# The latents' attention of a four-block network: where the first values and the last output projections are computed

## The reference

```python
h = jnp.concatenate([x, latents], axis=1)
q = (x @ q_w + q_b).reshape(b, 512, NH, DH)
kv = (h @ kv_w + kv_b).reshape(b, 576, NH, DH, 2)
kmat, v = (kv[..., 0], kv[..., 1])
attn = jnp.einsum('bkhd,bnhd->bhkn', q, kmat) / DH
attn = jax.nn.softmax(jnp.where(mask, attn, -inf), axis=-1)
attn_out = jnp.einsum('bhkn,bnhd->bkhd', attn, v).reshape(b, 512, H)
attn_out = attn_out @ out_w + out_b + residual
# then root mean square norm, an MLP with 2048 hidden channels, and the residual
```

## Time and profile before

| | us |
|---|---|
| median of three runs | 2801.22 (2800.64 to 2805.96) |
| the profiled execution | 2802.86, its span 2800.8 |
| TensorE busy | 2650.6 (95%) |
| VectorE busy | 1450.7 (52%) |
| ScalarE busy | 781.3 (28%) |
| GpSimd busy | 389.2 (14%) |
| mean granted TensorE clock | 0.98 of full speed |

### The profile page before, as it was taken

One profiled execution on the slowest core, in us unless ns is written; L12 is line 12 of the kernel. 1 busy time (PEld: TensorE's weight loads), 2 busy tenths in 40 slices (PEclk: granted clock), 3 DMA queues, 4 the chain that ended last, 5 costly groups with the idle time before them and its releaser, 6 DMA issues. The chain is left out here.

```text
span 2800.8 us, 30410 instructions
## 1 busy us (share of the span) xinstructions
PE 2650.6 (95%) x12328; PEld 1929.1 (69%) x12328; DVE 1450.7 (52%) x2282; ACT 781.3 (28%) x1363; POOL 389.2 (14%) x282
## 2 busy tenths in 40 slices
PE   9999999999899999879999999979999888899999
PEld 7778777877678888635444444358888766578887
DVE  6465566555763443435445454475334497763443
ACT  4322233223321110215344352430111143331110
POOL 0000000000220000014344342422000220220000
PEclk9999999999999999989999999899999999999999
DMA  4100110010100000321212122120000100100001
GB/s 190 60 31 32 59 61 31 32 60 1 64 1 31 31 1 1 135 56 45 52 39 64 49 49 55 33 106 32 18 16 0 68 1 0 52 14 30 31 1 60
DMA packets 35604, 118.28 MB, mean 42 GB/s; under 512 B 8069, under 2 KB 8198, under 8 KB 25994
## 3 DMA queue, kind: packets, MB, share of 16 engines
q1 hardware_dynamic: 35466, 116.35, 12.6%
HBM read 81.18 MB, written 7.34 MB: 32 GB/s over the span
## 5 line engine op out<-in xcount | busy, mean ns | idle before, releaser
L1549 DVE TENSOR_REDUCE l_top<-l_slot 128x1 f32<-128x512 f32 x256 | 170.3, 678 | 192.6 <-PE l_slot L1360 191.8
L1499 ACT ACTIVATE l_weighed<-l_across 128x512 f32<-128x512 f32 (+1 forms) x320 | 183.0, 594 | 298.1 <-PE l_across L1382 294.2
L389 PE MATMUL l_wide<-l_key_map,l_norm 128*128 128x260 f32 x1024 | 235.3, 383 | 2.7 <-ACT l_norm L544 2.3
L389 PEld LDWEIGHTS l_wide<-l_key_map,l_norm 128*128 128x128 f32 x1024 | 191.8, 190 | 32.1 <-ACT l_norm L544 2.7
L1230 POOL TENSOR_TENSOR l_paired<-l_weighed 128x2048 f32<-128x2048 f32 x32 | 145.5, 4548 | 397.2 <-ACT l_weighed L1499 337.0
L1382 PE MATMUL l_across<-l_q_stack,l_k_stack 99*128 99x512 f32 (+1 forms) x320 | 186.9, 588 | 11.8 <-ACT l_weighed L1499 8.8
L725 DVE TENSOR_TENSOR x<-l_added,x 128x512 f32<-128x512 f32 x128 | 87.0, 687 | 82.3 <-PE l_added L131 60.6
L1382 PEld LDWEIGHTS l_across<-l_q_stack,l_k_stack 99*128 99x128 f32 (+1 forms) x320 | 59.1, 186 | 97.0 <-issue 61.8
L1360 PE MATMUL l_slot<-l_k_stack,l_q_stack 97*128 97x512 f32 x256 | 112.0, 438 | 14.4 <-DMA l_k_stack<-l_k_parts 6.2
L2337 ACT ACTIVATE l0m_hidden<-l0m_up,columns 128x512 f32<-128x512 f32 x64 | 44.2, 692 | 271.7 <-PE l0m_up L131 259.6
L2337 ACT ACTIVATE l3m_hidden<-l3m_up,columns 128x512 f32<-128x512 f32 x64 | 44.2, 692 | 269.9 <-PE l3m_up L131 256.7
(11 more groups left out here) (379 smaller groups left out, 5943.0 us busy)
## 6 DMA issues: line engine op xcount, KB each, us to landing
l_k_stack<-l_k_parts SPq DMA_DIRECT2D x192, 72.0 KB, 2.0
l_q_stack<-l_q_parts SPq DMA_DIRECT2D x192, 64.0 KB, 2.0
l_wk<-in_weights SPq DMA_DIRECT2D x9, 1024.0 KB, 4.9
l_wv<-in_weights SPq DMA_DIRECT2D x9, 1024.0 KB, 4.8
l_wo<-in_weights SPq DMA_DIRECT2D x9, 1024.0 KB, 4.8
l_wqT<-in_weights SPq DMA_DIRECT2D x8, 1024.0 KB, 7.0
l0m_raw<-in_weights SPq DMA_DIRECT2D x8, 1024.0 KB, 4.7
l2m_raw<-in_weights SPq DMA_DIRECT2D x8, 1024.0 KB, 4.8
```

The costliest lines, as they stand in the source:

```text
L389: last = pe.matmul(wide[:, j, 0:W], norm[:, k, at:at + P], key_map[:, k, b, :, :].rearrange("p h c -> p (h c)"), start=k == 0, stop=k == K ...
L1499: act.activation(weighed[0:height(c), (CHUNKS * g + c) % RING, j, :], across[0:height(c), use % 2, :], ACT.Exp)\
L1549: dve.tensor_reduce(top[:, t, j:j + 1], slot[:, i % 2, :], AX.X, ALU.max, negate=True).then_inc(s["top_ready"], 1)
```

## The change

- The semaphore `setup` is split in `bias_scaled` and `mask_ready`. ScalarE's first copies wait for neither; its first q take waits for the first, SyncE's first stack load for the second.
- Element 0's values no longer stand in one block. `first_values(piece)` is one product; four stand ahead of the logits of group 0, and one ahead of each of the 16 logits. They use the banks of `gathered`, `totals` and `across`, which are unused until group 0's loop. VectorE takes a chunk ahead of maxima 0, 4, 8 and 12 and the last behind maximum 15; `split(1)` moves from ahead of the maxima to behind maximum 12. The first logits wait for `k1_out` and `q_out`, the first `turn_tops` for all values.
- Element 2's output projection no longer stands between the values of element 3 and group 12's loop. `late_out` puts one product beside steps 0 to 3 and 8 to 11 of groups 13 and 14, in the bank `work`; VectorE adds behind maxima 5 and 13 of those groups. SyncE's store of these rows moves to group 14.
- Element 3's output projection puts its first twelve products beside the first 12 steps of group 15 (`last_out`), in four banks; the last four follow the last `mixed` (`finish_out`). GpSimd adds the bias for these rows in group 15, between the two pair sums, no longer in group 12.
- `mixed` has two buffers, by element.

The diff, cut to its core:

```diff
-        mixed = n.sbuf(f"{tag}_mixed", [P, GROUPS, S], F32, mem)
+        mixed = n.sbuf(f"{tag}_mixed", [P, 2, GROUPS, S], F32, mem)
...
+        FIRST_VALUE_BANK = (gathered[:, :], totals[:, :], across[:, 0, :], across[:, 1, :], gathered[:, :])
+        LAST_BANK = (slot_bank[0], slot_bank[1], slot_bank[2], work[:, :])
+        TAIL = ALL - GROUPS + 1
...
-            sp.wait_ge(s["setup"], 2)
+            sp.wait_ge(s["mask_ready"], 1)
...
-                if g % GROUPS == GROUPS - 1 and b + 1 < B:
+                if g == ALL - 2:
+                    sp.wait_ge(s["out_added"], TPB * (B - 1))
+                    sp.dma_start(n.dram["l2_rows"][:, (B - 2) * TPB:(B - 1) * TPB, :], rows[:, :, :]).then_inc(s["rows_stored"], 16)
+                elif g % GROUPS == GROUPS - 1 and b + 2 < B:
...
+                if g == ALL - 1:
+                    add_bias(b)
...
+            def first_values(piece):
+                c, k = piece // KT, piece % KT
+                if c == CHUNKS - 1 and k == 0:
+                    pe.wait_ge(s["values_out"], 1)
+                last = pe.matmul(FIRST_VALUE_BANK[c][0:height(c), :], source[:, k, keys_of(c)], wv[:, k, :], start=k == 0, stop=k == KT - 1)
+                if k == KT - 1:
+                    last.then_inc(s["values_done"], 1)
...
+            def late_out(g, step):
+                if step % 8 >= GROUPS or step >= TILES_OF:
+                    return
+                t, m = 2 * (g - TAIL) + step // 8, step % 8
+                if m == 0:
+                    if t:
+                        pe.wait_ge(s["out_added"], TPB * (B - 2) + t)
+                    else:
+                        pe.wait_ge(s["mixed_ready"], GROUPS * (B - 1))
+                        pe.wait_ge(s["k1_out"], ALL)
+                last = out_product(B - 2, t, m, work[:, :])
+                if m == GROUPS - 1:
+                    last.then_inc(s["out_done"], 1)
+
+            def last_out(step):
+                if step >= TPB * (GROUPS - 1):
+                    return
+                m, t = step // TPB, step % TPB
+                if step == 0:
+                    pe.wait_ge(s["top_ready"], TILES_OF * ALL)
+                    pe.wait_ge(s["ctx_top_ready"], 4 * ALL)
+                    pe.wait_ge(s["out_added"], TPB * (B - 1))
+                if t == 0:
+                    pe.wait_ge(s["mixed_ready"], GROUPS * (B - 1) + m + 1)
+                out_product(B - 1, t, m, LAST_BANK[t])
+
+            def finish_out():
+                pe.wait_ge(s["mixed_ready"], ALL)
+                for t in range(TPB):
+                    out_product(B - 1, t, GROUPS - 1, LAST_BANK[t]).then_inc(s["out_done"], 1)
...
-                        pe.wait_ge(s["values_out"], CHUNKS)
+                        pe.wait_ge(s["k1_out"], 2)
+                        pe.wait_ge(s["q_out"], 2)
...
+                else:
+                    pe.wait_ge(s["values_out"], CHUNKS)
...
-            project_values(0)
+            for piece in range(KT):
+                first_values(piece)
             for i in range(TILES_OF):
+                first_values(KT + i)
                 logits(0, i)
...
+                        elif g + 1 < ALL:
+                            late_out(g, TPB * c + j)
+                        else:
+                            last_out(TPB * c + j)
...
-                    if g + 1 < ALL:
-                        project_values(g // GROUPS + 1)
-                    project_out(g // GROUPS)
+                    b = g // GROUPS
+                    if b + 1 < B:
+                        project_values(b + 1)
+                    if b + 2 < B:
+                        project_out(b)
+            finish_out()
...
-            act.wait_ge(s["setup"], 2)
+            act.mul(bq_scaled[:, 0:GROUPS], n.columns[:, COLUMNS[f"{tag}_bq"]:COLUMNS[f"{tag}_bq"] + GROUPS], INV).then_inc(s["bias_scaled"], 1)
...
+            act.wait_ge(s["bias_scaled"], 1)
...
-                if b and m == 0:
-                    dve.wait_ge(s["out_done"], TPB * b)
-                dve.tensor_tensor(mixed[:, m, :], gathered[:, :], inverse[:, :], ALU.mult).then_inc(s["mixed_ready"], 1)
-
-            def add_out(b):
-                dve.wait_ge(s["rows_ready"], TPB * (b + 1))
-                for t in range(TPB):
-                    dve.wait_ge(s["out_done"], TPB * b + t + 1)
-                    dve.tensor_tensor(rows[:, t, :], slot_bank[OUT_BANK[t]], rows[:, t, :], ALU.add).then_inc(s["out_added"], 1)
+                if b >= 2 and m == 0:
+                    dve.wait_ge(s["out_done"], TPB * (b - 1))
+                dve.tensor_tensor(mixed[:, b % 2, m, :], gathered[:, :], inverse[:, :], ALU.mult).then_inc(s["mixed_ready"], 1)
...
             split(0)
-            take_values(0)
-            split(1)
             for i in range(TILES_OF):
+                if i % KT == 0:
+                    take_value(0, i // KT, FIRST_VALUE_BANK[i // KT])
                 maximum(0, i)
+                if i == 3 * KT:
+                    split(1)
+            take_value(0, CHUNKS - 1, FIRST_VALUE_BANK[CHUNKS - 1])
             split_tops(0)
...
+                    if TAIL <= g < ALL - 1 and i in (5, 13):
+                        add_out(B - 2, 2 * (g - TAIL) + i // 8, work[:, :])
...
-                        take_values(b + 1)
-                    add_out(b)
+                        for c in range(CHUNKS):
+                            take_value(b + 1, c, slot_bank[VALUE_BANK[c]])
+                    for t in range(TPB):
+                        if b + 2 < B:
+                            add_out(b, t, slot_bank[OUT_BANK[t]])
+                        elif b + 1 == B:
+                            add_out(b, t, LAST_BANK[t])
```

More of the change, by code:

```diff
@@ L1242, in split, with add_bias @@
                 pool.tensor_tensor(k_parts[:, 1, :], k, k_parts[:, 0, :].bitcast(F32), ALU.subtract).then_inc(s["parts_ready"], 1)
+            def add_bias(b):
+                if b:
+                    pool.wait_ge(s["rows_stored"], 16 * b)
+                for t in range(TPB):
+                    pool.tensor_tensor(rows[:, t, :], n.x[:, b * TPB + t, :], bo_row[:, :], ALU.add).then_inc(s["rows_ready"], 1)
             for g in range(ALL):
@@ L1251, in _ @@
                     pool.tensor_copy(source[:, :, S:KEYS], n.ctx_f[:, :, (b + 1) * C:(b + 2) * C]).then_inc(s["ctx_ready"], 1)
+                if g == ALL - 1:
+                    add_bias(b)
                 add_pair(g, 1)
-                if g % GROUPS == 0:
-                    if b:
-                        pool.wait_ge(s["rows_stored"], 16 * b)
-                    for t in range(TPB):
-                        pool.tensor_tensor(rows[:, t, :], n.x[:, b * TPB + t, :], bo_row[:, :], ALU.add).then_inc(s["rows_ready"], 1)
+                if g % GROUPS == 0 and b + 1 < B:
+                    add_bias(b)
         @block.tensor
@@ L1337, in project_out @@
                 for t in range(TPB):
[L1338 removed]
+                    if t < 3:
                         pe.wait_ge(s["values_out"], CHUNKS * (b + 1) + t + 3)
@@ L1342, in project_out, with out_product @@
                     for m in range(GROUPS):
-                        last = pe.matmul(slot_bank[OUT_BANK[t]], mixed[:, m, t * P:(t + 1) * P], wo[:, m, :],
-                                         start=m == 0, stop=m == GROUPS - 1)
+                        last = out_product(b, t, m, slot_bank[OUT_BANK[t]])
                     last.then_inc(s["out_done"], 1)
+            def out_product(b, t, m, bank):
+                return pe.matmul(bank, mixed[:, b % 2, m, t * P:(t + 1) * P], wo[:, m, :], start=m == 0, stop=m == GROUPS - 1)
+            def late_out(g, step):
[26 more added lines that the diff above has]
+                    out_product(B - 1, t, GROUPS - 1, LAST_BANK[t]).then_inc(s["out_done"], 1)
             def logits(g, i):
@@ L1524, in _ @@
             dve.wait_ge(s["consts_loaded"], 16 * 3)
-            dve.tensor_scalar(mask[:, :], keep[:, :], 0.0, -1e30, ALU.is_equal, ALU.mult).then_inc(s["setup"], 1)
+            dve.tensor_scalar(mask[:, :], keep[:, :], 0.0, -1e30, ALU.is_equal, ALU.mult).then_inc(s["mask_ready"], 1)
             dve.wait_ge(s["zeroed"], 5)
@@ L1538, in split, with take_value @@
                 dve.tensor_tensor(k_parts[:, 1, :], k, k_parts[:, 0, :].bitcast(F32), ALU.subtract).then_inc(s["parts_ready"], 1)
-            def take_values(b):
-                for c in range(CHUNKS):
-                    dve.wait_ge(s["values_done"], CHUNKS * b + c + 1)
-                    dve.tensor_tensor(values[0:height(c), c, :], slot_bank[VALUE_BANK[c]][0:height(c), :], bv_row[0:height(c), :], ALU.add)\
-                        .then_inc(s["values_out"], 1)
+            def take_value(b, c, bank):
+                dve.wait_ge(s["values_done"], CHUNKS * b + c + 1)
+                dve.tensor_tensor(values[0:height(c), c, :], bank[0:height(c), :], bv_row[0:height(c), :], ALU.add).then_inc(s["values_out"], 1)
             def maximum(g, i):
```

20 lines of the change are left out of this document (10 added, 10 removed).

## The result

The changed kernel takes 2777.16 us (median of four runs, 2774.51 to 2779.15), the kernel before beside it 2801.62 us. The ratio is 0.9909, with an interval of 0.9892 to 0.9926. The profiled execution took 2779.15 us, its span is 2777.1. The gain is 24.5 us where 30.5 were forecast.

What follows compares the result with a forecast made beforehand. TensorE, busy 95% of the span, was taken as the bound, with waits and slow stretches to fill. Front -12.7, boundary and loops -11.4, end -6.4 sum to -30.5: 2772.4 from the profiled 2802.9, stated as 2771; range 2764 to 2784.

Steps and rivals of the forecast that it cites:

- the likeliest case: Whole kernel: the forecast itself, 2771 us, within 2766 to 2776, chance 0.55.
- First copies: Block start: copies no longer wait for the mask, -7.2, and the first q product runs at full clock, -2.6; together -9.8.
- Values beside the logits: Group 0's first logits: value products fill 1.7 us of waiting and 1.2 lost to the clock, -2.9.
- The boundary: Element 2 to 3: sixteen output products no longer run alone ahead of group 12's loop, -13.4.
- Groups 13 and 14: Element 2's late products return here, eight per group: +1.0 each, +2.0 for both.
- the walk: Hand calculation of group 14's new loop, first product to fourth quarter's: 17.9 us instead of 16.85, group 13 the same.
- The last projection: Group 15 and end: first three quarters +5.6, mixes -1.8, four last products instead of sixteen -10.2; together -6.4.
- the sign that I named for being wrong: Later blocks changing by over 1 us; the clock's stretches moving into the late products was named beside it.
- Clock low in the new loops: Rival: groups 13 and 14 +3 each, +2.6 if the first q product stays slow; 2780 us, chance 0.25.
- Clock high: Rival: gains 1.8 at the last products and 1.5 in the chain behind the first logits; 2768 us, chance 0.10.
- No hiding: Rival: products wait behind stalled logits; front 0 for -2.9, loops +13.8 for +2.0; 2786 us, chance 0.06.
- Mix of banks: Rival: changing banks holds TensorE at 1.2 GHz in front, groups 13, 14 and 15; 2825 us, chance 0.02.

Runs made afterwards that it cites:

- the experiment: Changed kernel with element 0's values again in one block ahead of the first logits, in the new banks: 2780.35 us, ratio 0.9915.
- warm: Kernel before, with 64 transposes into an unused bank in TensorE's idle stretch before the first q product: 2806.45 us against 2802.83, ratio 1.0011.
- the four parts: Four runs, changed kernel with one part undone each: mask's wait, values' block, element 2's projection block, element 3's: 2783.82, 2780.35, 2785.48, 2779.66 us.

## Why the prediction held, and where it did not

The forecast was 2771, the time 2777: right in sign and inside the range of 2764 to 2784, but 6 us too low, and just outside the likeliest case's own 2766 to 2776.

**First copies: held.** Forecast -9.8; from the first transpose to the first value product it went from 29.86 to 19.73 us, -10.1. The q product came at 1193.30 and not at 1192.7, but the whole block started 0.7 later (1190.53 for 1189.79): behind the first transpose it came at 2.8, with 2.9 foretold. With the mask's wait back, 10.0 return. The stack did not bind: its first issue came at 1205.45 (forecast about 1205) and the first logits at 1214.20 (forecast 1214), without a wait.

**Values beside the logits: held.** 1.96 us per step with two products as foretold, group 0's loop at 1247.08 (forecast 1246.8), 3.1 us at its place by the experiment against 2.9. They were the two kinds of lost time that the window of the earlier trace rows shows, waiting and clock, and no product became cheaper.

**The boundary: held.** Forecast -13.4, measured -14.0 in all executions.

**Groups 13 and 14: the walk was right, the case too narrow.** By hand 17.9 us to the fourth quarter, measured 18.21 in both, at full clock. By parts, in group 13: the first quarter 5.8 (by hand 6.1), from there to the logits that wait for VectorE's third maximum 4.9 (4.5), to the mixes 5.7 (5.5), the mixes 1.85 (1.8). Timeline of VectorE in the second quarter, changed kernel, and TensorE's wait behind it:

```profile
1726.36 0.95 DVE L1627 RECIPROCAL l_inverse<-l_totals 128x128 f32<-128x128 f32 x1
1727.22 1.22 DVE L1607 TENSOR_REDUCE l_top<-l_slot 128x1 f32<-128x512 f32 x2
1728.36 0.95 DVE L1627 RECIPROCAL l_inverse<-l_totals 128x128 f32<-128x128 f32 x1
1729.22 0.63 DVE L1640 TENSOR_TENSOR l_rows<-l_work,l_rows 128x512 f32<-128x512 f32 x1
```

```profile
1730.59 0.47 PE L1409 MATMUL l_slot<-l_k_stack,l_q_stack 97*128 97x512 f32 x1 [1.03 <-DVE l_top L1607]
```

VectorE has no gap and TensorE waits 1.03 for it, as the walk had it. But I took one clock for this loop, while its executions split about evenly between 29.8 and 31.3 or more. The ten longer ones have a mean of 31.9, 2.1 more than the others; with 10 of 18 like that, the +2.7 of the two groups becomes +5.0 where I had +2.0. This is the term that was mis-sized, by some 3 us of the 6 on average over executions; in the profiled one it was +2.7.

**The last projection: held in each step.** First three quarters 13.3 (forecast 13.2), mixes 1.86 (1.8), GpSimd's gap 1.09 (1.1), first of the last products to the last add 5.93 (5.5), the whole -6.1 (-6.4).

**What the sum lacked.** It went by one profile of before and took everything else as fixed. The rest moves by 10 us between profiles of equal instructions, and the sign that I named for being wrong, a change of over 1 us in the later blocks, showed up (+3.5). It needs no cause in the change: `warm`, which has nothing of it, shows 961.2 there, and kernels that differ only at the front or end 957.4 to 961.9. That test was far too tight for this kernel. The sum also took every gain at a place, clock included, for a gain of the whole, and the runs do not bear that out (16 of 32 us for the four parts, nothing for `warm`). The remaining 3 us of the miss are of this size; their cause stays open.

**The rivals.** *Clock low in the new loops* happens, in some executions, at its place and near its price; its other half, a slow first q product, did not: it took 3.70 in all eleven profiles without the mask's wait. *Clock high* came only in small part: from the last of the first logits to group 0's loop it is 5.8 us instead of 6.2, while the last products ran at 0.62. *No hiding* is out: the front and the boundary gave their gains. *Mix of banks* is out: 42 us of the front with two products and logits in different banks per step ran at 1.00. The Trainium skill (TensorE: Matmul & The Clock Gate, A second HAM failure mode) warns of a clock that swings when groups of matmuls cycle through PSUM banks; this case's trace does not show it in these loops. Its rule that gaps throttle and dense work releases (the same page, What's actually happening, HAM oscillation) agrees in direction with the start, 6.28 us behind a wait of 8.16 and 3.70 behind one of 0.83, and with the transposes that kept it warm; what no run here bears out is that such a release lowers the total.

## What to carry to other kernels

Price a moved product by the idle and slow time that the target's window shows, not by its own duration: where TensorE was dense, its time only moved (spreading the late products), and where it waited, most of it was hidden (sixteen late products of 13.4 us added 2.7 at full clock). Behind a long wait price the slow clock too, but don't count on it in the total (`warm` shows none of its 2.6 us there), and look at more than one execution before you call a loop's clock. After moving work off the end of a chain, look at what the chain then waits for in one piece: here one multiplication of all four tiles, whose split into quarters gave another 4 us at its place.

## What the runs showed of the hardware beyond that

One and the same loop has a fast and a slow case: groups 13 and 14 take 29.8 us or 31.3 to 32.8, by whether the granted clock falls at the end of the second quarter, where TensorE waits for VectorE. The block's first transposes do it too: without the mask's wait the q product started 2.77 us behind the first of them in nine profiles and 4.32 in two. Transposes also keep the clock up: 64 of them in the start's wait left it at 1.00 where it had been at 0.50 from 1195 on. And VectorE pays little for working in small pieces: four reciprocals of 128 columns back to back and one multiplication of 512 take 3.39 and 0.69, 4.1 us; in turn with multiplications of 128 columns (0.95 and 0.29) a quarter comes every 1.19 us, 4.8 in all. The split costs VectorE 0.7 us and gains 4 at the end, because the products start behind the first quarter and keep the full clock.
